# Routing logits of a soft mixture of experts computed once and kept with the slots across partitions

## The reference, cut to what matters

```python
xn = rmsnorm(x, norm_gamma)                            # tokens
sn = rmsnorm(slot_embeds, slot_norm_gamma)             # 8 experts x 64 slots
logits = jnp.einsum('bnd,esd->bnes', xn, sn)           # 256 tokens x 512 slots, per sequence
dispatch = jax.nn.softmax(logits, axis=1)              # over the tokens
combine = jax.nn.softmax(logits.reshape(b, n, e * s), axis=-1)   # over the slots
slots = jnp.einsum('bnd,bnes->besd', xn, dispatch)
h = gelu(jnp.einsum('besd,edh->besh', slots, w1) + b1)
eo = (jnp.einsum('besh,ehd->besd', h, w2) + b2).reshape(b, e * s, DIM)
out = jnp.einsum('bmd,bnm->bnd', eo, combine)
```

## Time and profile before

| what | value |
|---|---|
| median of 3 runs | 1197.23 us (1195.18 to 1197.71) |
| the profiled execution's own time | 1197.39 us |
| its span in the profile | 1195.3 us |
| PE busy | 1150.4 us, 96% |
| DVE busy | 908.1 us, 76% |
| ACT busy | 796.4 us, 67% |
| POOL busy | 609.8 us, 51% |
| PE clock granted, mean | 0.995 of full |

### The profile page before, as it was taken

The page is one execution under the profiler, slowest core; times in us unless marked ns, Lnnn a source line. Parts: engine busy times, 40 slices in busy tenths (PEclk is TensorE's granted clock), DMA queues, the critical chain, the costliest instruction groups (busy, mean ns, idle before and its releaser), DMA issues.

```text
span 1195.3 us, 28261 instructions
## 1 busy us (share of the span) xinstructions
PE 1150.4 (96%) x10564; PEld 839.8 (70%) x10564; DVE 908.1 (76%) x1978; ACT 796.4 (67%) x1529; POOL 609.8 (51%) x650
## 2 busy tenths in 40 slices
...
DMA packets 17892, 16.97 MB, mean 14 GB/s; under 512 B 608, under 2 KB 16992, under 8 KB 17504
## 3 DMA queue, kind: packets, MB, share of 16 engines
...
## 4 chain that ended last, share of the span: by engine, by line
PE 87%; ACT 9%; issue 2%; DVE 1%; DMA 1%; POOL 0%; SPq 0%; ACTq 0%; DVEq 0%; POOLq 0%
PE bank L970 13%; PE bank L921 9%; PE bank L931 7%; PE bank_s L952 7%; PE bank L879 5%; PE bank L912 5%; PE bank L941 5%; PE bank L891 5%; PE bank L885 3%; PE bank L904 3%; PE bank L820 3%; PE bank L980 3%; PE bank L874 3%; PE bank L789 3%; PE bank L997 2%; PE bank_s L955 2%
## 5 line engine op out<-in xcount | busy, mean ns | idle before, releaser
L664 DVE TENSOR_TENSOR ret<-bank_s,k_sb 128x1536 f32<-128x1536 f32 x128 | 224.7, 1755 | 85.2 <-PE bank L970 45.3
L335 POOL TENSOR_TENSOR urs<-uvar,mhalf 128x16 f32<-128x16 f32 x64 | 194.9, 3046 | 132.9 <-DVE uvar L680 132.9
L330 POOL TENSOR_TENSOR ret_abs<-ret_abs 128x512 f32<-128x512 f32 x128 | 163.1, 1274 | 159.4 <-ACT ret_abs L475 159.3
L475 ACT ACTIVATE ret_abs<-ret 128x1536 f32<-128x1536 f32 x128 | 190.2, 1486 | 57.1 <-DVE ret L664 54.0
L921 PE MATMUL bank<-slotsT,w_sb 128*128 128x128 f32 x1024 | 133.2, 278 | 0.0
L931 PE MATMUL bank<-w_sb,hact 128*128 128x128 f32 x1024 | 129.0, 277 | 0.9 <-ACT hact L470 0.9
L931 PEld LDWEIGHTS bank<-w_sb,hact 128*128 128x128 f32 x1024 | 121.7, 192 | 8.9 <-issue 6.6
L921 PEld LDWEIGHTS bank<-slotsT,w_sb 128*128 128x128 f32 x1024 | 123.1, 192 | 5.1 <-issue 0.5
L970 PE MATMUL bank<-ret,vrow 128*32 128x256 f32 (+1 forms) x2048 | 109.4, 331 | 0.0
L324 POOL TENSOR_SCALAR km<-kT,k_sb 128x256 f32<-128x256 f32 x128 | 66.7, 530 | 66.6 <-DVE kT L647 66.6
L970 PEld LDWEIGHTS bank<-ret,vrow 128*32 128x32 f32 x2048 | 55.2, 109 | 57.9 <-POOL ret_abs L330 22.9
...
## 6 DMA issues: line engine op xcount, KB each, us to landing
...
k_sb<-consts SPq DMA_DIRECT2D x1, 530.0 KB, 3.8
...
```

Source lines behind the costliest of these rows:

```text
L330: pool.tensor_tensor(both[:, :, P:SEQ], both[:, :, P:SEQ], both[:, :, SEQ:3 * P], ALU.add)\
L335: pool.tensor_tensor(urs[:, j], uvar[:, j], mhalf[:], ALU.pow).then_inc(ready["urs"].sem, 1)
L475: act.activation(ret_abs[:, q % MR], ret[:, q % MR], ACT.Abs).then_inc(ready["ab"].sem, 1)
L664: dve.tensor_tensor(ret[:, q % MR], bank_s[:, :, 0:3 * P], causal.unsqueeze(1).broadcast_to([P, Q, 3 * P]), ALU.mult)\
```

## The change

- `L`, `Lm`, `E`, `CT` and `CTc` are gone. `LT` alone makes the logits, slots on the partitions, as two matmuls of 256 tokens per block instead of one of 512; the second sequence of a pair uses the slot rows with the two experts of a block swapped (`snT_turned`). `LTc` (ACT) copies each block to `cT`, and both softmaxes work from there: `LTm` and `DTe` read `cT` instead of the bank.
- The maximum over slots now lies across partitions. `mx` (DVE, three) takes the maximum of the four blocks, `mxT` (PE, four transposes) turns it, `rmax` (DVE) reduces it to one negated value per token, `rB` (PE, four transposes of a broadcast column) spreads it over all partitions, `rBc` (ACT) copies it. `cs` (DVE, four) adds it to `cT` in place and `ce` (ACT, four) takes the exponential in place.
- The sums over slots come from a column of ones that `eorow` gets as its 129th: `out` makes 129 columns per tile, in two banks, and `z` in two halves reads the sum from the bank.
- Loads are split: `early` (identity, the first 40 columns of the vectors, W_spin), `loaded1` (the other weights of layer 0), `loaded` (slot rows and the rest), and the slot work is put between tasks of pair 0 (`between`).
- `ORDER` and `BANK` are new throughout; `out1`, `gatedT`, `o`, `z`, `attn`, `zt`, `zg` and the last of `usq`, `rowd`, `urs` and `gated` now have age 2; the other tasks of layer 1, from `xn3` and `qk` on, have age 1, where before those from `xn3T` and `qk` to `DT` had age 0.

```diff
-    "PE": [("CT", 0, 1), ("quad", 4, 1), ("slots", 0, 1), ("g", 2, 1), ("g", 3, 1), ("slots", 1, 1),
...
+           ("quad", 0, 1), ("LT", 0, 1), ("LT", 1, 1), ("LT", 2, 1), ("quad", 1, 1), ("vg", 1, 1),
...
-        eorow = sb("eorow", E // 2, 2, C)
+        eorow = sb("eorow", E // 2, 2, C + 1)
...
-        def steps_of(tasks, order):
+        def steps_of(tasks, order, between=()):
 
             for step in range(pairs + ages):
                 for name, k, age in order:
                     p = step - age
                     if 0 <= p < pairs:
                         tasks[name](p, p % 2, k)
+                        if p == 0 and (name, k) in between:
...
             load_x(0)
-            sp.dma_start(k_sb[:], consts).then_inc(loaded.sem, 16)
-            sp.dma_start(w_sb[:], weights).then_inc(loaded.sem, 16)
-            sp.dma_start(v_sb[:], vectors).then_inc(loaded.sem, 16)
+            late_k, late_w, late_v = K_COLS["qdecay"][0], W_COLS["q1"][0], V_COLS["b2"][0]
+            sp.dma_start(k_sb[:, 0:late_k], consts[:, 0:late_k]).then_inc(early.sem, 16)
+            sp.dma_start(v_sb[:, 0:late_v], vectors[:, 0:late_v]).then_inc(early.sem, 16)
+            sp.dma_start(w_sb[:, 0:C], weights[:, 0:C]).then_inc(early.sem, 16)
+            sp.dma_start(w_sb[:, C:late_w], weights[:, C:late_w]).then_inc(loaded1.sem, 16)
             sp.dma_start(slot_sb[:], slot_rows).then_inc(loaded.sem, 16)
+            sp.dma_start(w_sb[:, late_w:], weights[:, late_w:]).then_inc(loaded.sem, 16)
+            sp.dma_start(k_sb[:, late_k:], consts[:, late_k:]).then_inc(loaded.sem, 16)
+            sp.dma_start(v_sb[:, late_v:], vectors[:, late_v:]).then_inc(loaded.sem, 16)
...
+            pool.memset(eorow[:, :, :, C:C + 1], 1.0).then_inc(ready["setup"].sem, 1)
...
-                since(act, filled["L"], p - 1, 3)
                 since(act, filled["LT"], p - 1, 3)
                 act.activation(xn3T[:], bank[:], ACT.Copy).then_inc(ready["xn3Tc"].sem, 1)
 
-            def E_(p, par, j):
-
-                bank = bank_of("L", p, j)
-                act.wait_ge(*ready["lmax"](p, j))
-                since(act, filled["CT"], *((p, j - 2) if j >= 2 else (p - 1, j + 2)))
-                act.activation(crow[:, j % 2], bank[:], ACT.Exp, bias=lmax[:, j:j + 1], accum_out=csum[par][:, j:j + 1])\
-                    .then_inc(ready["E"].sem, 1)
-
-            def CTc(p, par, j):
-                bank = bank_of("CT", p, j)
+            def LTc(p, par, m):
+                bank = bank_of("LT", p, m)
                 since(act, filled["out"], p - 1, 1)
-                act.activation(cT[:, :, j * P:(j + 1) * P], bank[:].rearrange("p (m n) -> p m n", m=4), ACT.Copy)\
-                    .then_inc(ready["CTc"].sem, 1)
+                act.activation(cT[:, m], bank[:], ACT.Copy).then_inc(ready["LTc"].sem, 1)
+
+            def rBc(p, par, k):
+                bank = bank_of("rB", p)
+                since(act, ready["cs"], p - 1, 3)
+                act.activation(rB[:], bank[:], ACT.Copy).then_inc(ready["rBc"].sem, 1)
+
+            def ce(p, par, m):
+                act.wait_ge(*ready["cs"](p, m))
+                act.activation(cT[:, m], cT[:, m], ACT.Exp).then_inc(ready["ce"].sem, 1)
 
             def DTe(p, par, m):
-
-                bank = bank_of("LT", p, m)
                 act.wait_ge(*ready["ltmax"](p, m))
                 since(act, filled["DT"], *((p, m - 2) if m >= 2 else (p - 1, m + 2)))
                 for b in range(2):
-                    ins = act.activation(dT[:, m % 2, b], bank[:, b * SEQ:(b + 1) * SEQ], ACT.Exp,
+                    ins = act.activation(dT[:, m % 2, b], cT[:, m, b * SEQ:(b + 1) * SEQ], ACT.Exp,
                                          bias=ltmax[:, m, b:b + 1], accum_out=dsum[:, m, b:b + 1])
...
-            dve.wait_ge(loaded.sem, 64)
+            dve.wait_ge(early.sem, 48)
...
-            def Lm(p, par, j):
-                bank = bank_of("L", p, j)
-                dve.tensor_reduce(lmax[:, j:j + 1], bank[:], X, ALU.max, negate=True).then_inc(ready["lmax"].sem, 1)
-
             def LTm(p, par, m):
-                bank = bank_of("LT", p, m)
-                dve.tensor_reduce(ltmax[:, m], bank[:].rearrange("p (b n) -> p b n", b=2), X, ALU.max, negate=True)\
+                dve.wait_ge(*ready["LTc"](p, m))
+                dve.tensor_reduce(ltmax[:, m], cT[:, m].rearrange("p (b n) -> p b n", b=2), X, ALU.max, negate=True)\
                    .then_inc(ready["ltmax"].sem, 1)
+
+            def mx_(p, par, i):
+                dve.wait_ge(*ready["LTc"](p, i + 1))
+                if i == 0:
+                    since(dve, filled["mxT"], p - 1)
+                else:
+                    dve.wait_ge(*ready["mx"](p, i - 1))
+                dve.tensor_tensor(mx[:], mx[:] if i else cT[:, 0], cT[:, i + 1], ALU.max).then_inc(ready["mx"].sem, 1)
+
+            def rmax_(p, par, k):
+                bank = bank_of("mxT", p)
+                since(dve, filled["rB"], p - 1)
+                dve.tensor_reduce(rmax[:], bank[:].rearrange("p (j s) -> p j s", j=TILES), X, ALU.max, negate=True)\
+                   .then_inc(ready["rmax"].sem, 1)
+
+            def cs(p, par, m):
+                dve.wait_ge(*ready["rBc"](p))
+                dve.wait_ge(*ready["DTe"](p, m))
+                dve.wait_ge(*ready["mx"](p, 2))
+                dve.tensor_tensor(cT[:, m], cT[:, m], rB[:], ALU.add).then_inc(ready["cs"].sem, 1)
...
-            def z_(p, par, k):
-
-                dve.reciprocal(crec[:], csum[par][:]).then_inc(ready["crec"].sem, 1)
-                dve.wait_ge(*ready["crec"](p))
-                dve.wait_ge(*filled["out"](p, 1))
-                dve.tensor_tensor(z[:], banks[BANK["out", 0]][:].rearrange("p (j c) -> p j c", j=TILES),
-                                  crec[:].unsqueeze(2).broadcast_to([P, TILES, C]), ALU.mult).then_inc(ready["z"].sem, 1)
+            def z_(p, par, b):
+                dve.wait_ge(*filled["out"](p, b))
+                bank = banks[BANK["out", b]][:, 0:2 * (C + 1)].rearrange("p (j c) -> p j c", j=2)
+                tiles = slice(2 * b, 2 * b + 2)
+                dve.reciprocal(crec[:, tiles], bank[:, :, C]).then_inc(ready["crec"].sem, 1)
+                dve.wait_ge(*ready["crec"](p, b))
+                dve.tensor_tensor(z[:, tiles], bank[:, :, 0:C], crec[:, tiles].unsqueeze(2).broadcast_to([P, 2, C]), ALU.mult)\
+                   .then_inc(ready["z"].sem, 1)
...
-            def L(p, par, j):
-                pe.wait_ge(*ready["xn3Tc"](p))
-                bank = claim("L", p, j)
-                pe.matmul(bank[:], xn3T[:, j * P:(j + 1) * P], (snT[:], snT_turned)[j // 2], start=True, stop=True)\
-                  .then_inc(filled["L"].sem, 1)
-
             def LT(p, par, m):
                 pe.wait_ge(*ready["xn3Tc"](p))
                 bank = claim("LT", p, m)
-                pe.matmul(bank[:], snT[:, m * P:(m + 1) * P], xn3T[:], start=True, stop=True).then_inc(filled["LT"].sem, 1)
-
-            def CT(p, par, j):
-                pe.wait_ge(*ready["E"](p, j))
-                bank = claim("CT", p, j)
-                for m in range(4):
-                    ins = pe.transpose(bank[:, m * P:(m + 1) * P], crow[:, j % 2, m * P:(m + 1) * P], ident)
-                ins.then_inc(filled["CT"].sem, 1)
+                for b in range(2):
+                    ins = pe.matmul(bank[:, b * SEQ:(b + 1) * SEQ], (snT[:], snT_turned)[b][:, m * P:(m + 1) * P],
+                                    xn3T[:, b * SEQ:(b + 1) * SEQ], start=True, stop=True)
+                ins.then_inc(filled["LT"].sem, 1)
+
+            def mxT(p, par, k):
+                pe.wait_ge(*ready["mx"](p, 2))
+                bank = claim("mxT", p)
+                for j in range(TILES):
+                    ins = pe.transpose(bank[:, j * P:(j + 1) * P], mx[:, j * P:(j + 1) * P], ident)
+                ins.then_inc(filled["mxT"].sem, 1)
+
+            def rB_(p, par, k):
+                pe.wait_ge(*ready["rmax"](p))
+                bank = claim("rB", p)
+                for j in range(TILES):
+                    ins = pe.transpose(bank[:, j * P:(j + 1) * P], rmax[:, j:j + 1].broadcast_to([P, P]), ident)
+                ins.then_inc(filled["rB"].sem, 1)
...
-            def out_(p, par, i):
-                if i == 0:
-                    pe.wait_ge(*ready["CTc"](p, 3))
-                    pe.wait_ge(*ready["eoc"](p, E // 2 - 1))
-                    claim("out", p)
-                for j in (2 * i, 2 * i + 1):
+            def out_(p, par, b):
+                pe.wait_ge(*ready["ce"](p, 3))
+                pe.wait_ge(*ready["eoc"](p, E // 2 - 1))
+                bank = claim("out", p, b)
+                for i in range(2):
+                    j = 2 * b + i
                     for m in range(E // 2):
-                        ins = pe.matmul(banks[BANK["out", 0]][:, j * P:(j + 1) * P], cT[:, m, j * P:(j + 1) * P],
```

(16 more changed lines are left out.)

158 lines of the change are left out of this document (84 added, 74 removed), and 50 rows, old and new, of tables (BANK, ORDER, READ_BY).

## The result

The changed kernel takes 1119.71 us (median of 4 runs, 1119.05 to 1120.04); the kernel before, run beside it, 1196.89 (4 runs). The ratio is 0.9356, 95% interval 0.934 to 0.9372: 77 us faster. The forecast was 1127, range 1104 to 1160. The profiled execution has a span of 1118.0 us.

The account below looks back on a forecast made before the run. PE's instruction stream was taken to bound the kernel: 37.1 us of start, 66.9 for the second step, 947.8 for fourteen of 67.7, 59.0 and a tail of 14.3 make 1125.1 of span, plus 2.1: 1127 us, range 1104 to 1160.

Parts of the forecast that it names:

- Rival 3: DVE becomes the bound, nine two-input instructions each waiting for a whole add: step 77.7 us, time 1277; chance 0.05.
- PE's sum: PE's work removed and added per middle step, -5.10 us: 71.48 becomes 66.4 us if PE never waits.
- xnT waits for xn: PE waits before the next pair's xnT for DVE's queue from ret2 to xn: 0 to 1.2 us, taken 0.75.
- out0 waits for eoc3: PE waits at out0, whose eorow needs eo7 copied by eoc3: 0.3 to 0.5 us a step, taken 0.4.
- Small bank waits: PE waits at banks that come free within 0.1 us of their claim (score1, h5): 0.2 us a step.
- DVE's new work: Three mx, four cs, rmax and longer z, less four Lm: DVE's busy time from 56.5 to 59.6 us a step.
- the mean over chance meetings: Seven new DVE instructions meeting POOL's adds: 0.7 us of DVE a step, mostly in slack; bounds none or 8.9.
- The start: First statistic at 5 us, xnT at 9.2, then 27.7 and 0.2 for slot work: xn2T ends at 37.1.
- Second step: 67.7 us less 4.5 of PE work not there yet, plus 3.7 for half-speed PE and a copy: 66.9.
- pair 15 alone: The step with only this pair loses 10.3 us of PE work, 1.6 given back for thinner cover: 59.0 us.
- tail: From out0 to the end, grown by work moved a step later, two urs in a row among it: 14.3 us.
- Rival 2: Longer waits: PE catches DVE's late queue and half of the two-input losses, 3.5 us; step 71.2, time 1179; chance 0.17.

Follow-up runs that it names:

- lt_twice: The changed kernel with each LT task doing its two PE matmuls twice: 1172.96 us, 53.3 more.
- xn_alone: The changed kernel with add 3 moved behind dn 3 on POOL, out of the way of DVE's xn: 1129.49 us.
- mx_twice: The changed kernel with one more DVE maximum of 384 columns in front of each of the three mx: 1141.78 us, 22.1 more.
- banks: The changed kernel with row2, out0 and out1 in other banks, so that row2's has no reader in eoc2: 1119.6 us.

## Why the prediction was right, and by how much each term was off

The range held, and PE is the bound, as said. Of the terms of the step the largest error is in the one that no rival doubted, PE's own sum.

- **PE bounds the step before and after.** Right: lt_twice turns 3.46 us of PE work into 3.33 of time. Rival 3 didn't happen; DVE is busy 57.9 us a step, 9 less than the period.
- **PE's sum, 66.4 us.** The typical step of 67.04 less 0.79 at xnT, 0.28 at out0 and 0.19 at h5 is 65.8: 0.6 too high. (Its items add up to -5.07 instead of -5.10, which changes nothing.) Two parts of the 0.6 are in the rows. First, at CT2 and CT3 the kernel before lost more than the 0.34 that were taken out (below): from CT2 to gatedT 1.38 us for 0.89 and from gatedT on 0.49 for 0.44, so 0.54. Second, a change of kind costs on both sides. I had priced only the group ahead of it; the ordinary matmuls behind a quad or a g take 0.10 more too, as vg1 behind a quad and vg2 behind gatedT show (0.96 and 0.86). I find 13 such places in a step before and 9 after, some 0.4 us in all, an estimate from the rows, since four transposes lose only 0.05.

```profile
617.35 1.04 PE L897 MATMUL bank<-k_sb,crow 128*128 128x128 f32 x8
618.73 0.63 PE L989 MATMUL bank<-k_sb,gated 128*128 128x128 f32 x4 [0.34 <-ACT cT L442]
619.22 3.81 PE L941 MATMUL bank<-eorow,cT 128*128 128x128 f32 x32
```

```profile
584.88 1.13 PE L915 MATMUL bank<-w_sb,xn2T 128*128 128x512 f32 x2
585.84 0.60 PE L1029 MATMUL bank<-k_sb,gated 128*128 128x128 f32 x4
586.28 1.02 PE L915 MATMUL bank<-w_sb,xn2T 128*128 128x512 f32 x2
587.14 0.59 PE L922 MATMUL bank<-xn3T,snT 128*128 128x256 f32 x2
```

- **xnT waits for xn, 0.75 us.** Right in place and size: 0.57 listed, 0.79 by the starts. The cause is right in part. xn meets an add, as taken, and xn_alone shows what the meeting costs. But the walk began with ret2 waiting for g0, and in the trace ret2 follows drec without a gap. The chain leaves PE behind quad 1 and runs through DVE's queue from ret1 on, 5.5 us ahead of ret2, and mx_twice bears that out.
- **out0 waits for eoc3, 0.4 us.** Right in place, measured 0.28. The banks run corrected me: I had read it as row2's wait.
- **Small bank waits, 0.2 us.** PE's list has none in a typical step, but the starts show 0.19 round h5, one of the two places named.
- **DVE's new work.** Busy 57.9 instead of 59.6. Beside the seven new two-input instructions I hadn't counted what ends: zg meets no add (0.685) where it took 1.39, the two mix take 0.750 each for 0.969, LTm from `cT` takes 0.672 for 0.686, ret 1.747 for 1.755. Together 1.3 us a pair. And durations aren't busy time: the groups' durations grow by 2.5 us a pair, busy by 1.4, since neighbours overlap. Of the seven one meets an add, always the same: a table of order makes a collision happen in all steps or in none, so the mean over chance meetings (0.7 us a step) gave 0.54 but said nothing of where. It was taken to fall mostly in DVE's slack, and the mx that meets the add stands on the chain.
- **The start, xn2T's end at 37.1 us.** Measured 38.42. The miss is the table load, which ran during the loads before and stands behind xnT's transposes now.
- **The rest.** Second step 67.2 (66.9), pair 15 alone 58.6 (59.0), tail 14.7 (14.3). In front of the first xn2T PE waits 7.01 us, and from 37.30 to 44.00 its granted clock is 0.50, as it was before from 49.20 to 56.00; four transposes take 1.12 us there in both, as priced.

The sum was 7.1 us too high in the span: +1.3 at the start, +0.3, -8.7 in fourteen steps of 0.62, -0.4 and +0.4. The term that was mis-sized is PE's sum, 0.6 of the 0.7 by which a typical step came out shorter; out0 is the other 0.1, and xnT and the small waits are right to 0.04.

Rival 2's 3.5 us a step don't follow from its words: half of the bound of 8.9 would be 4.4. It didn't happen either way.

The tail shows one thing more (POOL and DVE, after):

```profile
1102.82 5.97 POOL L344 TENSOR_TENSOR urs<-uvar,mhalf 128x16 f32<-128x16 f32 x2 [5.64 <-DVE uvar L686]
```

```profile
1108.83 0.42 DVE L692 TENSOR_TENSOR gated<-ug,urs 128x256 f32<-128x256 f32 x1 [2.43 <-POOL urs L344]
```

The two urs one after the other are 6 us of the 14.7, as forecast; DVE sits idle 2.43 us of them and PE 3.56 us in front of gatedT1.
